# Softmax attention in query quarters: dense outputs by way of main memory, division on GpSimd, scores 14 tiles behind the row maxima

## The reference

```
q, k = rope(norm(x) @ Wq.T + bq), rope(norm(x) @ Wk.T + bk)
v = norm(x) @ Wv.T + bv
p = exp((q @ k.T - rowmax) / sqrt(8));  o = (p @ v) / sum(p)
x = x + concat_heads(o) @ Wo.T + bo
```

## Time and profile before

| | us |
|---|---|
| median of 3 runs (lowest, highest) | 855.79 (855.08, 859.73) |
| the profiled execution | 860.77 |
| span of its instructions | 859.0 |
| softmax attention layer, from its barrier to the next | 398 to 761.7 in the span |
| VectorE's 256 maxima tiles | 423.2 to 720.4 |
| busy in the span: PE, DVE, ACT, POOL | 715.8, 658.8, 526.6, 238.3 |

### The profile page before, as it was taken

One profiled execution on the slowest core, in us unless ns is written; L12 is line 12 of the kernel. 1 busy time (PEld: TensorE's weight loads), 2 busy tenths in 40 slices (PEclk: granted clock), 3 DMA queues, 4 the chain that ended last, 5 costly groups with the idle time before them and its releaser, 6 DMA issues. The chain is left out here.

```text
span 859.0 us, 20505 instructions
## 1 busy us (share of the span) xinstructions
PE 715.8 (83%) x8024; PEld 359.3 (42%) x8024; DVE 658.8 (77%) x1317; ACT 526.6 (61%) x1028; POOL 238.3 (28%) x295
## 2 busy tenths in 40 slices
PE   5999978887736999963989999999999999946880
PEld 2333236553426999961412222222222222236770
DVE  7887985446875555537799999999999999664555
ACT  3763622365713444425629999999999999624453
POOL 0130010204216767552473300100000100006773
PEclk9999989997856999985958999999999999767995
DMA  3440010000082311221756650403300000032123
GB/s 101 98 100 3 1 24 5 4 3 1 0 302 95 110 48 50 38 61 60 205 129 148 170 126 2 88 16 75 73 16 2 2 2 9 4 128 84 50 50 101
DMA packets 40968, 55.47 MB, mean 65 GB/s; under 512 B 9210, under 2 KB 31234, under 8 KB 40490
## 3 DMA queue, kind: packets, MB, share of 16 engines
q1 hardware_dynamic: 36906, 46.04, 20.1%
q0 software_dynamic: 3968, 8.13, 3.5%
HBM read 35.22 MB, written 14.55 MB: 58 GB/s over the span
## 5 line engine op out<-in xcount | busy, mean ns | idle before, releaser
L1063 DVE TENSOR_REDUCE arena<-psum 128x1 f32<-128x1024 f32 x256 | 292.8, 1217 | 10.4 <-PE psum L932 10.4
L1201 ACT ACTIVATE arena<-psum 128x512 f32<-128x512 f32 x512 | 276.5, 597 | 18.7 <-PE psum L961 11.4
L932 PE MATMUL psum<-arena 56*128 56x512 bf16 x512 | 164.5, 404 | 4.7 <-DVE arena L1063 3.6
L974 PE MATMUL psum<-arena 128*32 128x256 f32 (+1 forms) x1944 | 163.4, 408 | 5.9 <-issue 5.9
L961 PE MATMUL psum<-arena 59*128 59x512 bf16 x512 | 158.4, 390 | 0.1
L369 PE MATMUL psum<-arena 128*128 128x128 f32 x808 | 108.1, 281 | 0.4 <-DVE arena L420 0.4
L369 PEld LDWEIGHTS psum<-arena 128*128 128x128 f32 x808 | 102.0, 198 | 0.7 <-DVE arena L420 0.7
L974 PEld LDWEIGHTS psum<-arena 128*32 128x32 f32 x1944 | 38.8, 108 | 107.5 <-issue 61.6
L932 PEld LDWEIGHTS psum<-arena 56*128 56x128 bf16 x512 | 28.9, 95 | 115.6 <-DVE arena L1063 97.9
L485 POOL DMA_INDIRECT rows_y<-arena x62 | 62.6, 1009 | 37.7 <-DVE arena L434 31.9
L396 PE MATMUL psum<-arena 128*128 (+1 forms) x496 | 66.5, 277 | 2.8 <-ACT arena L464 2.0
(11 more groups left out here) (314 smaller groups left out, 1059.5 us busy)
## 6 DMA issues: line engine op xcount, KB each, us to landing
arena<-scr_q SPq DMA_DIRECT2D x32, 224.0 KB
arena<-scr_k SPq DMA_DIRECT2D x15, 448.0 KB
arena<-in_f_up SPq DMA_DIRECT2D x1, 4096.0 KB, 14.0
arena<-rows_y SPq DMA_DIRECT2D x12, 256.0 KB, 4.8
scr_q<-arena SPq DMA_DIRECT2D x6, 384.0 KB, 5.3
arena<-in_f_down SPq DMA_DIRECT2D x1, 2048.0 KB, 17.0
arena<-in_f_up SPq DMA_DIRECT2D x1, 2048.0 KB, 9.4
rows_x<-xn SPq DMA_DIRECT2D x5, 256.0 KB, 13.0
```

Source lines behind the costliest of these rows:

```text
L932: mm = pe.matmul(ps[:, bank + half, :], q[rows, k, qh, h, qt * P:(qt + 1) * P], kk[rows, k, h, half * BLK:(half + 1) * BLK], start=True, s ...
L974: mm = pe.matmul(ps[32 * h:32 * h + 32, 7, at], va[:, kb, (st % NG) * HG + h, :], pt[:, (u % 3) * HG + h, at], start=kb == 0 and half != 1 ...
L1063: dve.tensor_reduce(mx[:, qh, h * 4 + qt:h * 4 + qt + 1], ps[:, bank:bank + 2, :].rearrange("p a b -> p (a b)"), X, ALU.max).then_inc(S("a ...
L1201: act.activation(pt[:, (u % 3) * HG + h, :], ps[:, bank_of(i), :], ACT.Exp, scale=float(HD) ** -0.5).then_inc(S("a1_exp"), 1)
```

## The change

The query unit `e` becomes a quarter of 256 queries (32 units of `TE` = 8 maxima tiles; `UE` = 4 iterations). Each `scores` call fills a bank with two heads by 256 queries, in two matmuls of 256 columns, and an iteration covers two key blocks of one quarter. Maxima run 14 tiles in front instead of 22. The sums of the exponentials come out in eight rows per head (v gets eight columns of ones), ACT copies 256 columns per unit to `a1_o` (`output`), SP writes each unit to main memory (`put_by`) and reads it back as dense rows of outputs and of sums (`collect`), and POOL divides (`divide`: power -1, one Newton step, multiply; five instructions of 256 columns). Units 28 to 31 do not go through memory: PE gathers their rows by a product with a 0/1 matrix (`pick`), and VectorE divides those 32 rows. VectorE's 16 transposes with their reciprocals, and the four transposes back, are gone. q is loaded in four quarters of 112 KB (packets of 512 bytes instead of 1024) instead of two halves; a later group is issued after `max_rows(e)` for e = 7, 11, 15, 19. The three remaining bf16 splits on ACT move (`leading`, `following`), POOL interleaves `split_rows` with its rotations, and Wo is no longer reordered. The core of the diff:

```diff
-AHEAD = 22
+QW, TE, UE = 256, 8, 4
+QE = TILES // TE
+AHEAD = 14
...
-    return n // 32, n % 32 // 16, n % 16 // 4, n % 4
+    return n // 32, n % 32 // TE, n % TE // 2, n % 2
...
+    def scores(u, j):
+        st, e, kb = u // U, u // UE, 2 * (u % UE) + j // 2
+        k, i = st % NG, TAKEN["score", u * HG + j]
+        if j == 0 and u % U == 0:
+            pe.wait_ge(S(f"a1_two{st}"), 5 * 16)
+        if j == 0 and u % UE == 0:
+            pe.wait_ge(S(f"a1_mrow{e % 2}"), 16 * (e // 2 + 1))
         free_bank(i)
+        for x in range(2):
+            h = 2 * (j % 2) + x
+            mm = pe.matmul(ps[:, bank_of(i), x * QW:(x + 1) * QW], kk[0:KA, k, h, kb * P:(kb + 1) * P],
+                           q[0:KA, k, e % 4, h, :], start=True, stop=True)
+        mm.then_inc(S("a1_s2"), 1)
+
+    def values(u, i):
+        st, e, kb = u // U, u // UE, 2 * (u % UE) + i
+        if kb == 0:
+            pe.wait_ge(S("a1_va"), st + 1)
+            if e:
+                pe.wait_ge(S("a1_o"), e)
+        pe.wait_ge(S("a1_exp"), TAKEN["score", u * HG + 2 * i + 1] + 1)
         for h in range(HG):
+            mm = pe.matmul(ps[32 * h:32 * h + 32, 7, 0:QW], va[:, kb, (st % NG) * HG + h, :],
+                           pt[:, (u % 3) * HG + 2 * i + h // 2, h % 2 * QW:(h % 2 + 1) * QW],
+                           start=kb == 0, stop=kb == NTB - 1, skip_group_check=True)
+        if i == 1:
             mm.then_inc(S("a1_pv"), 1)
 
...
+    def pick(e):
+        pe.wait_ge(S("a1_o"), e + 1)
+        if e == QE - 3:
+            pe.wait_ge(S("a1_last"), 1)
+        elif e > QE - 3:
+            pe.wait_ge(S("a1_added"), e - QE + 4)
+        else:
+            pe.wait_ge(S("a1_red"), TILES)
+        part = o[:, e // 2, e % 2 * QW:(e % 2 + 1) * QW]
+        for k in range(2):
+            mm = pe.matmul(ps[96:128, 4 if e == QE - 2 else 3, k * QW:(k + 1) * QW], m["a1_sel"][:, k * 32:(k + 1) * 32], part,
+                           start=True, stop=True)
+        mm.then_inc(S("a1_pick"), 1)
+
+    def project_out(b, halves=range(2)):
+        if b == 0:
+            pe.wait_ge(S("a1_red"), TILES)
+        if b == 1:
+            pe.wait_ge(S("a1_added"), 1)
+        for n in halves:
+            pe.wait_ge(S("a1_div"), 2 * b + n + 1)
+            if b >= 2:
+                pe.wait_ge(S("a1_last"), 2 if b == 2 else 3 + n)
+            for j in (2 * n, 2 * n + 1):
+                mm = pe.matmul(ps[:, 4 - b // 2 if b < 3 else 4, j * D:(j + 1) * D], xnT[:, (b * TPB + j) * P:(b * TPB + j + 1) * P],
+                               m["a1_wo"][:], start=True, stop=True)
+        if halves[-1] == 1:
+            mm.then_inc(S("a1_out"), 1)
...
-            if u >= 2 and (beside or i == 0):
-                values(u - 2, i if beside else None)
-            if i == 0 and u % NTB == NTB - 2 and u + 2 < G * U:
-                turn_rows((u + 2) // NTB)
-        if u in OUT_UNITS:
-            project_out(OUT_UNITS[u])
-    values(G * U - 2)
-    project_out(2)
-    values(G * U - 1)
-    project_out(3)
+            if u >= 2:
+                values(u - 2, i)
+            if i == 0 and u % UE == UE - 2 and u + 2 < G * U:
+                turn_rows((u + 2) // UE)
+        if u == G * U - 7:
+            project_out(0)
+            pick(QE - 4)
+        if u == G * U - 6:
+            project_out(1)
+        if u == G * U - 5:
+            pick(QE - 3)
+        if u == G * U - 3:
+            project_out(2)
+    values(G * U - 2, 0)
+    values(G * U - 2, 1)
+    pick(QE - 2)
+    values(G * U - 1, 0)
+    values(G * U - 1, 1)
+    project_out(3, (0,))
+    pick(QE - 1)
+    project_out(3, (1,))
...
+    def divide(n):
+        k = n - 4
+        bank, at, of = 4 if n == 6 else 3, slice(n * QW, (n + 1) * QW), slice(96, P)
+        dve.wait_ge(S("a1_pick"), k + 1)
+        dve_step(c, dve.reciprocal(sums[of, at], ps[of, bank, QW:2 * QW]))
+        dve.tensor_tensor(dense[of, at], ps[of, bank, 0:QW], sums[of, at], ALU.mult).then_inc(S("a1_last"), 1)
...
+    add_out(0)
+    divide(4)
+    add_out(1)
+    divide(5)
     add_out(2)
     mv, rs, most = c.mem["mv"], c.mem["rs"], slice(0, 3 * TPB)
     dve.wait_ge(own.sem, own.n)
     dve.tensor_scalar(rs[:, most], mv[:, most, 1], 1e-5, None, ALU.add).then_inc(S("a1_nvar"), 1)
+    divide(6)
     dve.wait_ge(S("a1_nroot"), 1)
     dve_step(c, dve.reciprocal(rs[:, most], rs[:, most]))
     at = slice(TPB, 3 * TPB)
     dve.scalar_tensor_tensor(m["a1_off"][:], mv[:, at, 0], -1.0, rs[:, at], ALU.mult, ALU.mult).then_inc(S("a1_noff"), 1)
+    divide(7)
...
+    def output(e):
+        act.wait_ge(S("a1_pv"), (e + 1) * UE)
+        act.copy(o[:, e // 2, e % 2 * QW:(e % 2 + 1) * QW], ps[:, 7, 0:QW]).then_inc(S("a1_o"), 1)
...
+        if u in (0, 8, 16):
+            leading(5 + u // 8)
+        if u in (2, 11, 19):
+            following(5 + u // 8)
+        if u > 1 and u % UE == 1:
+            output(u // UE - 1)
+    output(QE - 1)
...
+    def divide(n, rows):
+        at = slice(n * QW, (n + 1) * QW)
+        pool.wait_ge(S(f"a1_dense{n}"), 2 * 16 * (NG if rows == P else NG - 1))
+        d, r, t = sums[0:rows, at], m["a1_r"][0:rows, 0], m["a1_r"][0:rows, 1]
+        pool_step(c, pool.tensor_tensor(r, d, m["a1_less"][0:rows, :].broadcast_to([rows, QW]), ALU.pow))
+        pool_step(c, pool.tensor_tensor(t, d, r, ALU.mult))
+        pool_step(c, pool.tensor_scalar(t, t, -1.0, 2.0, ALU.mult, ALU.add))
+        pool_step(c, pool.tensor_tensor(r, r, t, ALU.mult))
+        pool.tensor_tensor(dense[0:rows, at], dense[0:rows, at], r, ALU.mult).then_inc(S("a1_div"), 1)
+        pool.wait_ge(S("a1_div"), n + 1)
...
+        if e >= 12 and e % 4 == 0 and e // 4 + 1 < G:
+            values(e // 4 + 1)
+        if 18 <= e < 22:
+            divide(e - 18, P)
+        if e in (QE - 3, QE - 2):
+            divide(e - QE + 7, 96)
+    divide(6, 96)
+    divide(7, 96)
...
+    def put_by(e):
+        sp.wait_ge(S("a1_o"), e + 1)
+        sp.dma_start(outs[e], o[:, e // 2, e % 2 * QW:(e % 2 + 1) * QW]).then_inc(S(f"a1_by{e % 2}"), 16)
+
+    def collect(e):
+        g, n = e // 4 % NG, e // 16 * 4 + e % 4
+        to, at = slice(g * HG * HD, (g + 1) * HG * HD), slice(n * QW, (n + 1) * QW)
+        part = outs[e].rearrange("(h r) t -> h r t", r=32)
+        sp.wait_ge(S(f"a1_by{e % 2}"), 16 * (e // 2 + 1))
+        sp.dma_start(dense[to, at], part[:, 0:HD, :]).then_inc(S(f"a1_dense{n}"), 16)
+        sp.dma_start(sums[to, at], part[:, HD:2 * HD, :]).then_inc(S(f"a1_dense{n}"), 16)
...
+    for e in range(7, QE):
         max_rows(e)
-        if e == 3:
+        if e - 3 < QE - 4:
+            put_by(e - 3)
+        collect(e - 4)
+        if e == 7:
             for n in range(4, 8):
                 sp.wait_ge(S(f"a1_st{n}"), 48)
-        if e % 2 == 1 and e // 2 + 3 < G:
-            g = e // 2 + 3
+        if e % 4 == 3 and e // 4 + 3 < G:
+            g = e // 4 + 3
             sp.wait_ge(S("a1_s1"), 32 * (g - NG + 1))
             group(S1B, g, f"a1_one{g}")
             sp.wait_ge(S("a1_pv"), U * (g - NG + 1))
             group(0, g, f"a1_two{g}")
```

More of the change, by code:

```diff
@@ L818, in evictions @@
         out.append(("score", n))
-        if n % HG == 1 and n // HG % NTB == NTB - 2 and n // HG + 2 < G * U:
-            out.append(("rows", (n // HG + 2) // NTB))
+        if n % HG == 1 and n // HG % UE == UE - 2 and n // HG + 2 < G * U:
+            out.append(("rows", (n // HG + 2) // UE))
     return out
@@ L931, in max_half @@
         rows = slice(S1B, S1B + KR)
-        mm = pe.matmul(ps[:, bank + half, :], q[rows, k, qh, h, qt * P:(qt + 1) * P],
+        mm = pe.matmul(ps[:, bank + half, :], q[rows, k, qq, h, qt * P:(qt + 1) * P],
                        kk[rows, k, h, half * BLK:(half + 1) * BLK], start=True, stop=True)
@@ L949, in turn_rows @@
         free_bank(i)
-        pe.matmul(ps[0:3 * HG * 4, bank_of(i), 0:P], m["a1_ms"][:].rearrange("p i a -> p (i a)"), m["a1_id"][:],
+        pe.matmul(ps[0:3 * TE, bank_of(i), 0:P], m["a1_ms"][:].rearrange("p i a -> p (i a)"), m["a1_id"][:],
                   start=True, stop=True).then_inc(S("a1_s2"), 1)
[L953 to L959, removed]
-        free_bank(i)
-        pe.matmul(ps[:, bank_of(i), :], kk[0:KA, k, h, kb * P:(kb + 1) * P],
-                  q[0:KA, k, qh, h, :], start=True, stop=True).then_inc(S("a1_s2"), 1)
@@ L1182, in attn1_act @@
     biased(7)
-    for n in (4, 5):
-        leading(n)
-        following(n)
+    leading(4)
+    following(4)
     def rows(e):
@@ L1201, in attn1_act @@
             act.activation(pt[:, (u % 3) * HG + h, :], ps[:, bank_of(i), :], ACT.Exp, scale=float(HD) ** -0.5).then_inc(S("a1_exp"), 1)
[L1202 to L1214 removed]
+            if h == 1 and u % UE == UE - 2 and u + 2 < G * U:
+                rows((u + 2) // UE)
+        if u in (0, 8, 16):
[5 more added lines that the diff above has]
+    output(QE - 1)
     table_ahead(c)
@@ L1372, in attn1_sp @@
     group(0, 0, "a1_two0")
+    max_rows(0)
     group(S1B, 1, "a1_one1")
```

(42 more changed lines are left out.)

157 lines of the change are left out of this document (51 added, 106 removed).

## The result

The changed kernel takes 1148.62 us in the median against 855.88 of the kernel before, a ratio of 1.341 (95% interval 1.337 to 1.345). I had said 861. The profiled execution has a span of 1147.6 us at a mean granted clock of 0.803; the layer's 256 maxima tiles took 500 us, where they took 297, and from the last of them to the layer's end it is 129 us, where it was 41.

A forecast was written before the change was run, and what follows sets the result against it. VectorE and PE were taken to tie at 18.4 us per 16 tiles, with PE and ACT setting the pace behind the maxima. Terms -9.5 - 0.6 + 1.4 + 0 + 1.5 + 12 + 0 = +4.8 on 855.8 gave 861; 8-in-10 range 846 to 876.

The forecast's parts named there:

- The power of POOL: In POOL's divide: power from 0.72 to 9 us, whole divide 3.8 to 12, taken as 6, hidden, cost 0.
- rival D: On POOL: the power is slow and split_rows comes late, +14 to +20, near 876; chance 0.12.
- The rule for what is hidden: On POOL: a divide before split 19 to 22, 30 and 31 must fit into 9.2 - 1.4 = 7.8 us.
- The queue of SP: Maxima rows wait behind a group's load at units 8, 12, 16, 20: 4 x 3.0 = 12 lost, bounds 0 and 20.
- A: Whole kernel: the author's own forecast, 861, range 856 to 867; chance 0.45.
- Rival C: In the loop: each 3.3 us gap of PE makes its clock fall, up to 16 more, 11 taken: 872; chance 0.15.
- Rival B: At SP's loads: queue delay small, load ends by t + 12 or small DMA overtakes: 849; chance 0.28.
- The shorter tail: Behind the maxima: lag of 14 tiles instead of 22, 23.3 us instead of 32.8, 9.5 gained.
- the layer's end: From the last values to the layer's end: 7.9 us instead of 8.5, 0.6 gained.
- Quarter units: In the maxima loop: twice as many units, 9.25 us per eight tiles against 9.205, 1.4 lost.
- split scores: On PE: two score matmuls of 256 columns for one of 512, cost 0, bound above 7 in all.
- startup: Start of the layer: scores begin eight tiles earlier, ACT's moved splits fall near copies of bank 7, 1.5 lost (0 to 4).

The follow-up runs named there:

- experiment 1: Changed kernel with the power of POOL's divide replaced by a product of the same operands: 871.94 us, ratio 1.018.
- experiment 8: Changed kernel, loads spread, the power replaced on POOL by a first guess from the bits of s and three Newton steps: 849.62 us, ratio 0.994.
- experiments 4 to 6: Changed kernel: power in divides 0 to 3 only, 1014.6 us; loads spread and power on 32 of 256 columns, 855.1 us, or on 64, 889.79 us.
- experiment 5: Changed kernel, loads spread, the power on 32 of its 256 columns after a memset of 0.5: 855.1 us, ratio 1.000.
- experiments 9 and 10: Changed kernel, product for power, maxima rows of units 8 to 31 issued from GpSimd's queue: ratio 1.022 with loads in one lump, 1.031 with loads spread.
- experiment 2: Changed kernel, product for power, second half of a group's load moved two units later: 851.21 us, ratio 0.993.
- experiment 3: Changed kernel, the eight powers given different widths, partitions and exponents, a memset of 0.5 for the rest: 1004.01 us in one execution.
- experiment 7: Changed kernel, loads spread, VectorE takes the reciprocals in place of POOL's power and Newton step: 860.96 us, ratio 1.006.

## Why the prediction was wrong, point by point

- **The power of POOL: the failed step.** The power was bounded "from 0.72 if it is like a product to 9 us at the 35 ns a column of the dearest POOL row", and of the whole `divide` it says "I take 6, nearer the arithmetic rows, hidden, cost 0". The direction of rival D was right, its price wrong: 41.1 us each (159.5 ns a column), eight times, 277 us of the 293 (experiment 1). The upper bound was no bound. It took the dearest row of the trace for the dearest that the engine can do, and a memset of 32 columns says nothing of a power. Nor were its 35 ns a price for a column: in experiment 5 a memset of 256 columns takes 0.31 us. I wrote that nothing in the trace prices it, and gave it 0.12 and a width of 20 us. The rule for what is hidden (free time 7.8 us) was right: experiment 8 fills 7.6 and leaves 0.33, and experiments 4 to 6 follow it. The 0.8 of grace that I added to it did not show: the divide of 8.9 us already costs 5.5.
- **The queue of SP: right in place, cause and length of the gaps; the clock behind them was a second failed term.** "4 x 3.0 = 12 lost": gaps of 2.4 to 3.5 at exactly those four units, 11.3 of idle time in all. With the fallen clock they cost 20 in the trace and 21.6 between the two kernels, so each costs 5 to 5.4, where A had 3 and C 5.75. Rival C was nearly right, and my reason against it, that PE is full before and after, does not hold: PE is full before the gap, idle for 3.8, and then runs at half the clock, as the windows of the changed kernel show:
```profile
508.00:512.00 4.00, 3.83 (x52) 1.66 (x49) 3.94 (x4) 3.80 (x9) 0.00 (x0) 1.00 1.01 191
...
516.00:518.00 2.00, 0.99 (x9) 0.48 (x13) 0.34 (x1) 0.37 (x1) 0.00 (x0) 0.50 0.20 58
518.00:520.00 2.00, 2.00 (x19) 0.65 (x22) 0.89 (x1) 1.10 (x3) 0.00 (x0) 0.50 0.00 0
```
  Rival B, a small delay, is excluded. In the changed kernel's own trace SP's order at unit 8 reads as I had it; the rows stand behind the ten issues of the load:
```profile
507.20 0.31 SPq L1373 DMA_DIRECT2D arena<-scr_k  x1
507.57 2.26 SPq L1373 DMA_DIRECT2D arena<-scr_q  x4
509.87 0.79 SPq L1387 DMA_DIRECT2D arena<-arena  x1
```
  PE has done all else by 513.2, and its next score starts at 517.01:
```profile
517.01 0.37 PE L964 MATMUL psum<-arena 59*128 59x256 bf16 x1 [3.81 <-issue]
```
  Counted from the rows before (500.37, the t of the sum), these rows are issued at t + 9.5 and wanted at t + 12.8, and the DMA engines are full until t + 16, where I had 9.2, 12.2 and 15. And the order of the ring, for which I had cited the Trainium skill ("DMA: Bandwidth & Descriptors", section "Queues, rings and completion order"), is not needed for the delay: experiments 9 and 10 have it on two queues, 7.5 and 5.4 us from issue to landing.
- **The shorter tail and the layer's end: right.** 31.2 was the sum; 31.4 was measured (experiment 2), with the clock at 1.00 until 744. Within it the last values end 22.5 behind the last maximum where I had 23.3, and the end takes 8.9 for 7.9. VectorE's reciprocal of 256 columns, which I had called short, is 1.76 us, twice in that path.
- **Quarter units, split scores, startup: right within a microsecond.** "1.4 + 0 + 1.5": the period is 9.29 (I had 9.25), the first seven periods are together 1.7 above that, and the tiles as a whole take 1.8 more for the 2.9 taken. Score matmuls of 256 columns cost nothing visible. The rule of the Trainium skill on weight loads ("TensorE: Matmul & The Clock Gate", section "LDWEIGHTS (loading the stationary operand)"), which I had set aside, would have made the tiles 45 us longer; they became 1.8 longer.
- **The rest together.** With the power a product, the chip takes 871.94, where my terms give 861 and rival C, with the clock, 872; with the queue out too, 851.21 for 849. Two small slips in the working move nothing: 18.22 / 16 is 1.14 and not 1.13, and 3 x 1.107 + 0.2 is 3.5 and not 3.6.

## What to carry to other kernels

An operation that no row of the trace shows has no upper bound from the other rows; before it goes eight times into an engine's order, time it once at two widths. In-order work beside a loop was free here up to the engine's idle time in one period and cost about one for one beyond it, so measure that idle time first and look for arithmetic that fits it (a `divide` with a seed and three Newton steps took 7.6 us where one with the power took 44). A small DMA that the next step waits for is best issued well before a large one, not beside it; here a second queue gave it no way around.

## What the hardware showed that I had not expected

- GpSimd's two-input power costs 159.5 ns a column and 0.3 us, the same on 16 to 128 partitions and for exponents of 0, 1 and -1 (experiment 3); a product costs 2.8 ns a column.
- VectorE's reciprocal of 256 f32 columns takes 1.74 us from SBUF on 128 partitions (experiment 7) and 1.76 from PSUM on 32 (experiment 2), where a product of 32x256 takes 0.43.
- A gap of 3 us in a full PE is followed by some us at the 1.2 GHz level (0.50 from 516 to 522 us in the changed kernel), which costs about 2 us more.
- A DMA of 6 KB on GpSimd's queue took 7.5 and 5.4 us beside a load on SP's, and 2.1 with none (experiments 9 and 10).
